# The first tiles of a token tower's attention: gathers and roots in another order, table copies begun after tile 1's special rows

## The reference

```
h = concat(token_table[x], cat_table[x])              # (64, 128, 256)
h = h + attn(layernorm(h), W_qkv, b_qkv)
    # phi = elu + 1; kv = phi(k)^T v per head; phi(q) kv / (phi(q) . sum phi(k) + 1e-6), per row of x
h = h + ffn(layernorm(h), sim_matrix, gates, q_proj, k_proj, v_proj, o_proj)
    # cosine gating over 16 experts (relu, at least the top 2), q, k, v as weighted sums of expert
    # products, causal softmax attention over 128 tokens, o_proj of the experts, weighted again
```

## Time and profile before

| | |
|---|---|
| median of 3 runs | 1085.45 us (1084.37 to 1086.52) |
| the profiled execution | 1086.31 us, its span 1084.6 us |
| busy share of the span | PE 89%, PEld 82%, DVE 81%, POOL 65%, ACT 54% |
| instructions | 23702 |
| granted clock of PE, mean | 0.973 |
| DMA | 150.56 MB, mean 139 GB/s |

### The profile page before, as it was taken

How to read it: one execution, slowest core, us unless ns; L and a number is a source line. 1 busy time by engine, 2 the same in 40 slices (tenths; PEclk the granted TensorE clock), 3 DMA queues, 4 the chain that set the end, 5 groups by cost and what they waited for, 6 DMA issues and landing times.

```text
span 1084.6 us, 23702 instructions
## 1 busy us (share of the span) xinstructions
PE 966.7 (89%) x6831; PEld 892.9 (82%) x6831; DVE 873.4 (81%) x2889; ACT 582.9 (54%) x1569; POOL 700.0 (65%) x924
## 2 busy tenths in 40 slices
PE   0788999999999835999999599999999999999998
PEld 0677887878788725899999499999999999999997
DVE  2568999999999865655555279999999999999998
ACT  1456666666666512544444255555555555555554
POOL 6667777777777678000000378888888888888885
PEclk9989999999999967999999789999999999999999
DMA  6465334444333236888888423333333333332331
GB/s 199 137 191 153 124 127 147 152 146 127 124 125 118 89 126 205 279 285 260 255 262 257 150 78 98 93 95 91 91 98 94 94 90 91 99 98 86 86 98 35
DMA packets 132325, 150.56 MB, mean 139 GB/s; under 512 B 14708, under 2 KB 119650, under 8 KB 132196
## 3 DMA queue, kind: packets, MB, share of 16 engines
q1 hardware_dynamic: 112964, 97.59, 29.0%
q0 software_dynamic: 18080, 50.36, 15.6%
q10 hardware_dynamic: 1152, 1.05, 0.3%
HBM read 83.79 MB, written 78.88 MB: 150 GB/s over the span
## 4 chain that ended last, share of the span: by engine, by line
DVE 39%; PE 38%; issue 9%; POOL 6%; DMA 6%; ACT 1%; SPq 0%; POOLq 0%; DVEq 0%; ACTq 0%
PE bank L1431 12%; PE bank L1433 10%; PE bank L1432 10%; DVE w_attn L1414 5%; DVE qk_e L1368 4%; DVE row_x L1408 3%; PE bank L1438 3%; DVE phi L1120 3%; DVE x L1368 3%; POOL sorted_x L745 2%; DVE attn L1132 2%; DVE kvm L1153 2%; DMA h<-in_L_tok_special_table,ids 2%; DVE stats L1160 2%; DMA row_x<-in_L_tok_special_table,ids 2%
## 5 line engine op out<-in xcount | busy, mean ns | idle before, releaser
L1431 PE MATMUL bank<-wo_hi,split_lo 128*128 128x256 f32 x1024 | 304.6, 297 | 10.1 <-DVE x L1368 4.6
L1433 PE MATMUL bank<-wo_hi,split_hi 128*128 128x256 f32 x1024 | 288.8, 282 | 0.0
L1432 PE MATMUL bank<-wo_lo,split_hi 128*128 128x256 f32 x1024 | 288.5, 282 | 0.0
L1431 PEld LDWEIGHTS bank<-wo_hi,split_lo 128*128 128x128 f32 x1024 | 194.0, 189 | 23.6 <-DVE qk_e L1368 11.6
L1432 PEld LDWEIGHTS bank<-wo_lo,split_hi 128*128 128x128 f32 x1024 | 194.1, 190 | 0.0
L1433 PEld LDWEIGHTS bank<-wo_hi,split_hi 128*128 128x128 f32 x1024 | 193.6, 189 | 0.0
L940 ACT ACTIVATE h<-bank,rwo 128x256 f32<-128x256 f32 x256 | 107.5, 471 | 115.6 <-PE bank L1433 111.6
L818 POOL DMA_INDIRECT row_y<-sorted_y,pair_now x128 | 124.5, 972 | 31.2 <-issue 21.3
L811 POOL COPY pair_now<-pair_at 128x2 uint32<-128x2 uint32 x64 | 11.9, 186 | 178.0 <-SPq L599 178.0
L1269 DVE TENSOR_TENSOR split_lo<-bank,split_hi 128x256 fp32r<-128x256 f32 x144 | 60.8, 423 | 69.3 <-ACT split_hi L902 67.9
L1368 DVE SCALAR_TENSOR_TENSOR x<-bank,rwo,x 128x256 f32<-128x256 f32 x256 | 108.5, 473 | 2.7 <-PE bank L1433 1.9
(11 more groups left out here) (228 smaller groups left out, 2664.7 us busy)
## 6 DMA issues: line engine op xcount, KB each, us to landing
sorted_y<-row_y SPq DMA_DIRECT2D x36, 384.0 KB, 3.1
sorted_y<-w_attn SPq DMA_DIRECT2D x36, 384.0 KB, 3.1
row_x<-sorted_x SPq DMA_DIRECT2D x72, 128.0 KB, 2.9
h_rows<-h SPq DMA_DIRECT2D x64, 128.0 KB, 1.7
row_x<-h_rows SPq DMA_DIRECT2D x64, 128.0 KB, 2.2
out_h<-row_x SPq DMA_DIRECT2D x64, 128.0 KB, 1.7
embed_table<-in_L_tok_token_table SPq DMA_DIRECT2D x10, 625.0 KB
embed_table<-in_L_tok_special_table SPq DMA_DIRECT2D x10, 623.0 KB
```

Source lines behind the costliest of these rows:

```text
L1431: pe.matmul(ps, left[1][c], right[0][c], start=(c == 0), stop=False)
L1432: pe.matmul(ps, left[0][c], right[1][c], start=False, stop=False)
L1433: last = pe.matmul(ps, left[0][c], right[0][c], start=False, stop=(c == n - 1))
```

## The change

POOL: the wait for the small tables (small_loaded) moves from the start of the stage to just before the first small gather. Step c now issues token(c+7), small(c+7) and then special(c+8), where it issued small(c+6), special(c+7) and token(c+7); special(0) opens step -7. Roots 0 and 1 are formed in steps -6 and -5, between the small gather and the next special one; roots 2 and 3 in steps -3 and -2 ahead of the gathers; no root in step -1; from step 0 on, row c+4 at the head of the step, as before. sim_inv moves from step -5 to the end of step -1. DVE: simn moves from step -4 to step 0; the subtraction for w_attn stands after roots_in(0) in step -5; stats(1) moves from the end of step -5 into step -4, behind centers(0). SP: the first table copy waits until special(1) has landed.

```
@@ SP, step1
                 at = i.c - COPY_FROM
+                if at == 0:
+                    landed_quarter(sp, special_gathered, Tile(1))
                 if 0 <= at < COPY_STEPS:
@@ POOL
-            pool.wait_ge(small_loaded, 64)
...
+            def special_rows(tile):
+                if in_parts(tile):
+                    pool.indirect_dma_start(out=h[tile.c % 8][:, HALF:C], out_offset=None, in_=special_table,
+                                            in_offset=offsets(ids[:, tile.c, 1:2]),
+                                            bounds_check=N_SPECIAL - 1, oob_is_err=False
+                                            ).then_inc(special_gathered[tile.q], 16)
+            def token_rows(tile):
...
+            def small_rows(tile):
+                if in_parts(tile):
+                    if tile.c == 0:
+                        pool.wait_ge(small_loaded, 64)
+                    landed_quarter(pool, special_gathered, tile)
...
+            def form_roots(row):
                 if 0 <= row < N_ROOTS:
                     pool.wait_ge(done["roots_in"], row + 1)
                     pool.tensor_tensor(roots[:, row, :], roots_in[:, row, :], minus_half[:, 0:3], ALU.pow
                                        ).then_inc(done["roots"], 1)
...
+            def step1(i):
+                gather = i.shift(7)
+                if i.c == -7:
+                    special_rows(gather)
+                if i.c in (-3, -2):
+                    form_roots(i.c + 5)
+                elif i.c >= 0:
+                    form_roots(i.c + 4)
+                token_rows(gather)
+                small_rows(gather)
+                if i.c in (-6, -5):
+                    form_roots(i.c + 6)
+                special_rows(gather.shift(1))
+                if i.c == -1:
+                    pool.wait_ge(setup_v, 4)
+                    pool.tensor_tensor(sim_inv[:, :], sim_norm[:, :], minus_half[:, :], ALU.pow
+                                       ).then_inc(setup_p, 1)
+                if gather.inside(B) and not in_parts(gather):
                     if gather.c == JOINED_FROM:
                         pool.wait_ge(rows_joined, 16 * (2 * COPIES + 4))
@@ DVE
+            def row_stats(tile, slot):
+                rows_landed(dve, tile.c)
+                dve.bn_stats(stats[:, 2 * slot, :], h[tile.c % 8]).then_inc(done["ln1_stats"], 1)
             def step1(i):
-                if i.c == -5:
-                    dve.wait_ge(setup_a, 4)
-                    dve.tensor_tensor(w_attn_s[1], w_attn[:, :, :], w_attn_s[0].bitcast(F32), ALU.subtract
-                                      ).then_inc(setup_v, 1)
-                if i.c == -4:
+                if i.c == 0:
                     dve.wait_ge(setup_p, 1)
...
+                if i.c == -4:
+                    row_stats(Tile(1), 0)
...
+                if i.c == -5:
+                    dve.wait_ge(setup_a, 4)
+                    dve.tensor_tensor(w_attn_s[1], w_attn[:, :, :], w_attn_s[0].bitcast(F32), ALU.subtract
+                                      ).then_inc(setup_v, 1)
+                if stats_tile.inside(B) and i.c != -5:
+                    row_stats(stats_tile, 1 - i.p)
```

More of the change, by code:

```diff
@@ L703, in offsets @@
                 return bass.IndirectOffsetOnAxis(ap=index, axis=0)
[L705 to L712, removed]
+            def special_rows(tile):
[6 more added lines that the diff above has]
+                if in_parts(tile):
+                    pool.indirect_dma_start(out=h[tile.c % 8][:, 0:HALF], out_offset=None, in_=token_table,
+                                            in_offset=offsets(ids[:, tile.c, 0:1])
+                                            ).then_inc(rows_gathered[tile.q], 16)
+            def small_rows(tile):
+                if in_parts(tile):
+                    if tile.c == 0:
+                        pool.wait_ge(small_loaded, 64)
+                    landed_quarter(pool, special_gathered, tile)
+                    pool.indirect_dma_start(out=h[tile.c % 8][:, HALF:C], out_offset=None,
+                                            in_=category,
+                                            in_offset=offsets(ids[:, tile.c, 0:1]),
+                                            bounds_check=N_SMALL - 1, oob_is_err=False
+                                            ).then_inc(rows_gathered[tile.q], 16)
+            def form_roots(row):
                 if 0 <= row < N_ROOTS:
@@ L1174, in step1 @@
                         piece(g)
-                if stats_tile.inside(B):
-                    rows_landed(dve, stats_tile.c)
-                    dve.bn_stats(stats[:, 2 * (1 - i.p), :], h[stats_tile.c % 8]).then_inc(done["ln1_stats"], 1)
+                if i.c == -5:
[4 more added lines that the diff above has]
+                    row_stats(stats_tile, 1 - i.p)
             run1(dve, step1)
```

## The result

The changed kernel takes 1095.51 us (median of 4 runs, 1092.59 to 1097.71) against 1085.99 us before (median of 4): the ratio is 1.0087, 95% interval 1.006 to 1.0115, slower by about 9.5 us. That is the side that was forecast, at twice the size (4.9 us), and 0.5 us outside the range. The profiled execution took 1097.71 us, with a span of 1096.0; it was the slowest of its four, so its sums are read against its own time, 11.4 us above the profiled one of before.

What follows compares the result with a forecast made beforehand. The bound was taken to be the feed loop of special gather, landing, small gather, next special gather; +7.8 - 4.7 + 1.9 = +5.0 us, tail -0.1, gave +4.9: 1091.2 us (1090.3 against the median), range 1083.5 to 1095.

Steps and rivals of the forecast that it cites:

- H: Rival in e10's own forecast: the moved pow is hidden by special(6)'s landing or given back later; ratio within 1.001 of 1.
- part 1: Held-back table copies: specials 0 and 1 gain 5.3 us, specials 3 and 4 lose about 2.8 + 1.
- the walk: Start times stepped through on GpSimd and VectorE for the first tiles, ending with centers(4) at 58.4 against 50.62.
- forecast +7.8: Delay of centers(4), in us, behind root(4), which was queued after small(6), special(7) and the pow.
- what comes back, -4.7: Steps from centers(4) to centers(10): small-row stalls go, six steps at 5.3 give 31.8 us instead of 36.5.
- The clock's price: TensorE, idle for 9 us before step 0, then gets a clock of 0.50; +1.9 us over the next steps.
- The tail: After centers(10): rows 10 to 12 stay within 0.2 us, taken as -0.1, and the shift carries whole to the end.
- (a): Rival: the feed runs free, gathers land in about 3 us beside copies; centers(4) near 44.5, about 1079 us; chance 0.17.
- (b): Rival: delay and repair cancel, special(6) lands early, clock holds, stalls of steps 1 to 6 go; 1084 to 1087; chance 0.20.
- (c): Rival: held-back copies gain tile 0 nothing, special(0) takes 6.48 us; about 1092.3; chance 0.18 together with (d).
- (d): Rival: later-begun copies become the bound and hold tile 14's gather, 2 us; about 1092; chance 0.18 together with (c).

Runs made afterwards that it cites:

- e9: The kernel before with roots of rows 4 to 10 formed between special(c+7) and token(c+7) instead of at the step's head: ratio 1.0051, +5.5 us.
- e10: The kernel before with only the pow of sim at the end of step -1 and simn in step 0: ratio 1.0017, +1.8 us.
- e3: The changed kernel with rows 4 to 11 formed a step sooner, between token and small gather, pow left in step -1: ratio 1.0088, +9.6 us.
- e4: The changed kernel with the pow at the end of step -6 and rows 4 to 11 formed a step sooner: ratio 1.0043, +4.7 us.
- e1: The changed kernel without SP's wait, so that table copies start at once: ratio 1.0079 to the kernel before, +8.6 us.
- e6: The kernel before with only SP's wait for special(1) ahead of the table copies added: ratio 1.0012, +1.3 us.
- e5: The changed kernel with pow in step -6, rows 4 to 11 a step sooner, and no SP wait ahead of the copies: ratio 1.0013, +1.4 us.
- e7: The changed kernel with the 20 table copies in steps -2 to 6 instead of -7 to 6: ratio 1.0075, +8.1 us.

## Why the prediction was wrong, step by step

**Right.** The cause and its place: root(4) behind small(6), special(7) and the pow. e9 shows the first part of it by itself (+5.5), e10 gives the second +1.8, not clear of H; e3 and e4 show that both gates hold the same step. The first table copy came at 15.54 (forecast 15 to 16), the first x1 8.7 us sooner (centers(0) 18.32), centers(2) only 1.6 us sooner, an idle VectorE of 7.7 us before centers(4) (7.0 of them released by the pow through simn, which the prediction did not have), a clock of 0.50 behind it, and no wait for small rows after tile 5. That the held-back copies move the load to later gathers is borne out too, by e1 and e6.

**Wrong by its size: the landings of specials 4 and 5 (part 1 and the walk).** Part 1 set 5.3 us gained on specials 0 and 1 against 2.8 + 1 lost, a small gain in sum. Measured, 5.0 are gained (6.48 to 4.33, 5.43 to 2.53) and specials 3 to 6 lose 2.1 + 3.9 + 3.4 - 1.4 = 8.0; as a price in the whole, holding the copies back is a loss, of 0.8 us (e1, within the noise), 1.3 (e6) or 3.3 (e4 to e5). The walk let special(4) land in 3 to 4 us and special(5) before 44.4. They took 6.43 and 5.97. Special(4) landed at 39.9, and special(5), issued at 41.96, at 47.9. The step that failed is the statement that the copies drain at about 37 and leave special(5) a quiet queue: they lasted until about 39. The prediction knew that copies 9 and 10 hang on h2(0), which it put at about 41, but set them beside special(6) at 46.4. In the run h2(0) was stored at 39.81 and the two went out at 40.21 and 41.03, just ahead of special(5) at 41.96, which the long landing of special(4) had pushed behind them (the walk had it at 40.3). Small(5) so came 3.6 us later than in the walk (48.69 for 45.1). Special(6) landed in 3.55 us instead of 5.0, which gave 1.4 back. Centers(4): forecast +7.8, measured +9.8.

**Wrong in kind: what comes back, -4.7.** From centers(4) to centers(10) the changed kernel took 36.3 us, against 36.5 before and 33.7 forecast (31.8 and 1.9 for the clock). Up to centers(9), at 89.20, the forecast held: 28.8 us for 28.4. The clock's price fits: the two steps from 60.43 to 72.77 took 12.3, 1.7 above two at 5.3. The stalls on small rows did go. But the wait for a special gather did not; it moved from small rows, which VectorE waits for at the end of a step, to the roots, which it waits for at the head. Root(10) behind small(12), which waited 3.10 us for special(12), and special(13) held VectorE for 2.20 us at once, and the step to centers(10) took 7.5 us for 5.3. The prediction priced the new order on this queue for root(4) alone, and took it to be free for roots 5 to 11. e9 shows the same stall before centers(10) (2.45 us) with nothing else of the change in place, e3 that taking them out of the queue brings the small-row stall back (2.90 us). With -0.2 in place of -2.8, and +9.8 in place of +7.8, the sum is the +9.6 that was measured at centers(10); these two terms are the whole miss up to there.

**The tail** was right within half a microsecond: +9.1 at centers(12) and +9.3 at row 66, though tile 14's gather then waited 1.61 us for the last small table. One reading in it was off: before, tile 14's gather began 3.05 us after the last copy's issue (92.55 to 95.60), not some 2. The 9.5 us of the medians agree with that shift; the profiled pair differs by 11.4.

**The rivals.** (a) is out, by its own sign: specials 2 and 3 landed in 5.42 and 4.62 us, not within 3.4. (b) is out: nothing cancelled. (c) is out in its size: with w_attn alone beside it special(0) landed in 4.33 us, 1.8 above the quiet 2.53, and with the copies too in 6.48 (6.20 in e1). W_attn itself, issued at 5.79, had landed after 4.9 us, about when special(0) did. By the Trainium skill ("DMA: Bandwidth & Descriptors", Queues, rings and completion order) each DMA engine takes turns between its queues by packets; that w_attn alone costs something agrees with it, that it costs as much as w_attn and copies together was not seen. (d) came true in part, 1.61 us at 104.65, with no measurable cost in the sum.

**The parts.** Taken out of the changed kernel one after the other: pow and roots' place 4.7 (e4), then the held-back copies 3.3 (e5), and 1.4 is left. Put into the old kernel one by one: e6 +1.3, e9 +5.5, e10 +1.8, together 8.6 of 9.4. The two ways agree that the roots' place with the pow is the largest part (4.7 and 7.3); on its size and on the copies' share (3.3 and 1.3) they differ, by 2 to 3 us, which is about what the intervals leave open.

## What to carry to other kernels

When a gather is moved ahead in a hand-written queue, list for each wait what now stands behind it, for every step and not for the first alone: a wait moved off one consumer lands on the next instruction in the queue. A second gate of the same step (here simn behind the pow) hides what the first one's repair brings, so test the two together before one is called harmless. Holding a bulk copy back gains only if its bytes find an empty stretch later; here they met the next tiles' gathers.

## What had not been expected of the hardware

One special gather of 128 rows (64 KB) landed in 2.53 us alone, 4.33 beside w_attn's 768 KB, 4.6 to 6.5 in a row of table copies, and 7.37 beside just two copies (e7). GpSimd's power of -0.5 took 0.88 us for 3 values a partition and 2.96 for 16.

Stage 3 has two cycles that hold for hundreds of microseconds, 7.12 and 7.21 us a tile, and kernels that differ only in the order of work 600 us earlier fell into one or the other. In the slower one, from 800 to 900 us, VectorE's sum of two gathered rows takes 1.54 us in place of 1.09, and GpSimd is 88% busy in place of 84%. What selects it was not found; only that three of three kernels with special gathers two steps ahead, which are also those with the earliest end of stage 1, show it, each in its one profiled execution.

In the first 35 us the granted clock of the rows is no safe guide. In the kernel before, the matmuls of 512 columns start 0.43 us apart from 30.14 on (30.14, 30.56, 30.99), where the rows show 1.00; in the changed kernel they stand equally 0.43 us apart (32.86, 33.29, 33.72), and there the rows show 0.50.
